# Row maxima of the first batch from float32 keys and queries, and a prologue written out in a new order, in an attention and expert kernel

## What is computed

```
def reference(x, ctx_1024, mask_Bx1x1xS2_fk0, ...):
    # attention of layernorm(x) over ctx: 16 heads of 16
    q = split_heads(layernorm(x) @ Wq + bq); k = split_heads(ctx @ Wk + bk); v = split_heads(ctx @ Wv + bv)
    logits = einsum('bhqd,bhkd->bhqk', q, k) / sqrt(16) + mask * -1e9
    x = x + merge(softmax(logits) @ v) @ Wo + bo
    # router and experts
    scores = softmax(layernorm(x) @ w_gate); weights, idx = top_k(scores, 2)
    x = x + sum over k of weights[k] * expert[idx[k]](layernorm(x))     # capacity 1024
```

## Time and profile before

| | us |
|---|---|
| median of 3 runs | 433.39 (429.33 to 435.75) |
| the profiled execution | 432.8 |
| its span, first to last instruction | 430.7 |
| TensorE, VectorE, ScalarE busy | 370.0, 248.4, 214.0 |

### The profile page before, as it was taken

The page is one execution under the profiler, slowest core; times in us unless marked ns, Lnnn a source line. Parts: engine busy times, 40 slices in busy tenths (PEclk is TensorE's granted clock), DMA queues, the critical chain, the costliest instruction groups (busy, mean ns, idle before and its releaser), DMA issues.

```text
span 430.7 us, 9281 instructions
## 1 busy us (share of the span) xinstructions
PE 370.0 (86%) x2752; PEld 292.7 (68%) x2753; DVE 248.4 (58%) x693; ACT 214.0 (50%) x342; POOL 165.7 (38%) x174
## 2 busy tenths in 40 slices
PE   5437895898899999998988599989899999999990
PEld 3324663565566656665654399878699999999980
DVE  4636656589988988887878356752233332333320
ACT  2620474557466665744446568534244454544440
POOL 5020152342747658241253005742233334243332
PEclk9956699899999999999999699999899999999997
DMA  6589259387784949487136213554432332424330
GB/s 201 123 197 191 53 178 187 132 187 198 162 201 173 202 166 206 131 187 190 50 137 215 82 50 62 130 107 87 73 62 46 62 48 47 73 42 73 51 56 4
DMA packets 65468, 51.93 MB, mean 121 GB/s; under 512 B 11898, under 2 KB 62346, under 8 KB 65418
## 3 DMA queue, kind: packets, MB, share of 16 engines
q1 hardware_dynamic: 58028, 42.71, 40.6%
q0 software_dynamic: 7008, 8.43, 12.0%
q10 hardware_dynamic: 400, 0.40, 0.3%
HBM read 32.89 MB, written 19.06 MB: 121 GB/s over the span
## 4 chain that ended last, share of the span: by engine, by line
PE 55%; DMA 18%; DVE 9%; issue 7%; SPq 6%; ACT 3%; POOL 1%; POOLq 0%; ACTq 0%; DVEq 0%
PE bank L1032 19%; PE bank L1043 9%; DMA out<-CTt,GG 7%; PE bank L987 5%; DVE NEG L1170 5%; PE bank L875 5%; PE bank L958 4%; PE bank L919 3%; PE bank L892 3%; DMA wf<-NMT 3%; DMA wf<-qparts_d 3%; PE bank L971 3%; PE bank L883 2%; DMA slots<-R,slot 2%; PE bank L1012 2%
## 5 line engine op out<-in xcount | busy, mean ns | idle before, releaser
L1032 PEld LDWEIGHTS bank<-CX,KS 128*128 128x128 f32 x912 | 109.0, 194 | 6.4 <-issue 4.7
L1032 PE MATMUL bank<-CX,KS 128*128 128x128 f32 x912 | 109.9, 278 | 2.4 <-issue 2.3
L1170 DVE TENSOR_REDUCE NEG<-bank 128x2 f32<-128x512 f32 x128 | 85.7, 685 | 35.7 <-PE bank L958 34.3
L761 ACT ACTIVATE PR<-bank 128x512 f32<-128x512 f32 x128 | 73.2, 591 | 47.2 <-PE bank L971 46.5
L665 POOL DMA_INDIRECT out<-CTt,GG x38 | 58.9, 1549 | 97.6 <-DMA out<-CTt,GG 60.8
L801 ACT ACTIVATE KS<-wf 128x1536 f32 x40 | 59.2, 1483 | 43.1 <-PE bank L1032 42.6
L1398 DVE COPY CX<-bank 128x256 f32<-128x256 f32 x39 | 16.5, 424 | 77.2 <-PE bank L1012 77.2
L958 PE MATMUL bank<-KS,wf 99*128 99x256 bf16 x224 | 45.6, 290 | 15.9 <-DMA wf<-qparts_d 10.2
L1043 PE MATMUL bank<-wp,QF 128*128 x228 | 56.9, 386 | 2.4 <-DVE CTt L1412 2.4
L584 POOL DMA_INDIRECT slots<-R,slot x32 | 32.7, 1022 | 38.0 <-DVE slot L1276 26.5
L971 PE MATMUL bank<-wf,KS 102*128 102x256 bf16 x224 | 43.2, 273 | 3.9 <-DMA wf<-NMT 3.2
(11 more groups left out here) (171 smaller groups left out, 466.4 us busy)
## 6 DMA issues: line engine op xcount, KB each, us to landing
wf<-in_L_ffn_c_fc SPq DMA_DIRECT2D x8, 768.0 KB, 5.2
XG<-slots SPq DMA_DIRECT2D x40, 128.0 KB
kparts_d<-KP SPq DMA_DIRECT2D x8, 384.0 KB, 2.5
KS<-kparts_d SPq DMA_DIRECT2D x8, 384.0 KB
KS<-kparts_d SPq DMA_DIRECT2D x24, 128.0 KB
qparts_d<-QP SPq DMA_DIRECT2D x8, 384.0 KB, 3.1
wp<-in_L_ffn_c_proj SPq DMA_DIRECT2D x8, 384.0 KB, 4.9
wf<-qparts_d SPq DMA_DIRECT2D x7, 384.0 KB
```

What stands on the lines that cost most here:

```text
L761: act.activation(PR[:, s % NPROB, :], STB[s % 2][:], ACT.Exp).then_inc(exp_done, 1)
L1032: ins = pe.matmul(bank[2 + 2 * u + g][:, c * P:(c + 1) * P], UP[u][:, (k * 2 + g) * FF + c * P:(k * 2 + g) * FF + (c + 1) * P], XTG[:, u, ...
L1170: dve.tensor_reduce(NEG[:, n % 2, t, 2 * hp:2 * hp + 2], MXB[m % 2][:].rearrange("p (i s) -> p i s", i=2), AX.X, ALU.max, negate=True).the ...
```

## The change

Batch 0's row maxima no longer use the rows from DRAM. VectorE makes, from the float32 keys and queries of batch 0 in the layout of the projection, two copies each (`KZ`, `QZ`, in the space of later expert weights): in a group of 32 partitions, two heads, copy i keeps head i and has in the place of the other head the mask (`MK` on the keys' side, `mask_row` on the queries'). `direct_maxima` multiplies 32 partitions by 32 partitions, four groups into four banks, and `reduce_direct` takes the maxima. Its 32 matmuls take the place of the 32 of `row_max_logits(0, u)`. The rows of batch 0 are still made, for the logits.

Iterations -2 and -1 are gone. Each engine has a prologue written out by hand: order of loads, of projections, of parts. ScalarE issues the loads of mask and biases, the rows of `MK` and half 0 of the maxima's rows of batch 0. GpSimd makes the subtractions of batches 0 and 1. There are 14 matmuls with an unread result at the start. Batch 2 is projected from unit 0 of iteration 0 on (lead 0: CT 0, K 1, XT 5, Q 7, second parts 9 and 10), the 16 maxima of batch 1 are packed in units 5 to 15 (`FIRST_MAXIMA`), NM0 of batch 1 moves from unit 11 to 13. `stats1_of(3)` is taken ahead of VectorE's loop and was in iteration -1, `stats1_of(4)` moves to unit 15. X of batch 3 is loaded behind the query reads of batch 1, x of batches 4 to 7 in iteration 0 behind the reads of batch 2 and ahead of `max_rows(1, 0)`. The reads and writes of SyncE in the iterations are as before, in functions with new names.

```diff
-    "second K of the first": 2, "second Q of the first": 8, "start of 1": 7, "lead": 7, "lead of 2": 4,
+    "lead": 7, "lead of 2": 0,
...
-ITERATIONS = range(-2, B)
+ITERATIONS = range(B)
+FIRST_MISC = [("CT", 0), ("K", 0), ("XT", 0), ("Q", 0), ("CT", 1), ("XT", 1), ("K", 1), ("Q", 1), ("NM0", 0), ("V", 0)]
+AT_FIRST = {"NM0": 13, "split 0": 11, "stats1": 15}
+FIRST_MAXIMA = {5: 1, 6: 1, 7: 2, 8: 1, 9: 2, 10: 1, 11: 1, 12: 2, 13: 1, 14: 2, 15: 2}
+GROUPS = 4
...
+def maxima_at(it, u):
+
+    if it + 1 >= B:
+        return ()
+    if it > 0:
+        return (u,)
+    first = sum(FIRST_MAXIMA.get(w, 0) for w in range(u))
+    return range(first, first + FIRST_MAXIMA.get(u, 0))
...
+        DIRECT = (bank[0], bank[1], bank[4], bank[5])
...
+        KZ = ZSPACE[:, 0:2 * KC * S].rearrange("p (i c s) -> p i c s", i=2, c=KC)
+        QZ = ZSPACE[:, 2 * KC * S:4 * KC * S].rearrange("p (i c s) -> p i c s", i=2, c=KC)
+        MK = ZSPACE[:, 4 * KC * S:4 * KC * S + 2 * S].rearrange("p (i s) -> p i s", i=2)
...
-            sp.dma_start(bkc[:], bk.rearrange("(c p) -> p c", p=P), allow_slow_non_contiguous=True).then_inc(wk_in, 16)
+            load_rows(1)
...
-            load_rows(1)
             sp.dma_start(wv[:], Wv.rearrange("(k p) n -> p k n", p=P)).then_inc(wv_in, 16)
-            load_rows(2)
...
+            load_rows(2)
...
+            load_output_weights(0)
+            sp.wait_ge(mask_out, 16)
+            mask_rows(0)
+            mask_rows(1)
+            write_keys(0)
+            load_output_weights(1)
+            write_queries(0)
+            read_keys(0)
+            read_queries(0)
+            write_keys(1)
+            load_context(2)
+            write_queries(1)
+            read_keys(1)
+            load_output_weights(2)
+            read_queries(1)
+            load_rows(3)
+            load_output_weights(3)
+            load_router()
+            load_context(3)
             for it in ITERATIONS[:-1]:
-                if 0 <= it:
-                    max_rows(it, 1)
+                max_rows(it, 1)
...
+                if it == 0:
                     for m in range(4, B):
                         load_rows(m)
+                max_rows(it + 1, 0)
+                if it + 4 < B:
+                    load_context(it + 4)
+                load_weights(it)
...
+            pool.memset(MK, 0.0).then_inc(mk_zero, 1)
+            pool.wait_ge(mk_zero, 1)
...
+            layernorm1(0)
...
-            layernorm1(0)
             layernorm1(1)
+            split_keys(pool, 0)
+            split_queries(pool, 0)
+            split(pool, 1)
+            layernorm1(2)
+            normalize1(pool, 2)
...
+            act.dma_start(maskrow[:], mask.rearrange("b i j s -> b (i j s)")).then_inc(mask_in, 16)
+            act.dma_start(bkc[:], bk.rearrange("(c p) -> p c", p=P), allow_slow_non_contiguous=True).then_inc(bk_in, 16)
+            act.dma_start(bqc[:], bq.rearrange("(c p) -> p c", p=P), allow_slow_non_contiguous=True).then_inc(bq_in, 16)
...
+            for i in range(2):
+                act.dma_start(MK[DH * (1 - i):P:2 * DH, i, :],
+                              mask.rearrange("b i j s -> b (i j s)")[0:1, :].broadcast_to([GROUPS, S])).then_inc(mk_in, 16)
...
+                        if n == 0 and kind == "Q" and c == 0:
+                            ins.then_inc(q_half, 1)
...
+            evacuate("CT", 0)
+            evacuate("K", 0)
+            evacuate("XT", 0)
+            first_part("K", 0)
+            second_of_keys(0)
+            evacuate("Q", 0)
+            first_part("Q", 0)
+            evacuate("CT", 1)
+            evacuate("XT", 1)
+            second_of_queries(0)
+            evacuate("K", 1)
+            first_part("K", 1)
+            evacuate("Q", 1)
+            second_of_keys(1)
+            evacuate("NM0", 0)
+            act.wait_ge(nmt_ready[0], 1)
+            for j in range(3):
+                act.dma_start(query_rows(0)[R_MAX + j:R_MAX + j + 1, 0:8, :],
+                              NMT[8 * j:8 * j + 8, 0, :]).then_inc(nm_in[0], 16)
+            first_part("Q", 1)
+            second_of_queries(1)
+            evacuate("V", 0)
...
+                    pe.wait_ge(mx_reduced, UNITS)
...
+            def direct_maxima(c, t):
+
+                first = GROUPS * (TB * c + t)
+                if t == 0:
+                    pe.wait_ge(qz_ready, 2 * (c + 1))
+                if first == 0:
+                    pe.wait_ge(kz_ready, 2)
+                for i in range(2):
+                    for g in range(GROUPS):
+                        if i == 0 and first > 0:
+                            pe.wait_ge(mx_reduced, first - GROUPS + g + 1)
+                        rows = slice(2 * DH * g, 2 * DH * (g + 1))
+                        ins = pe.matmul(DIRECT[g][:, i * S:(i + 1) * S], QZ[rows, i, c, t * P:(t + 1) * P], KZ[rows, i, c, :],
+                                        start=True, stop=True)
+                        if i == 1:
+                            ins.then_inc(mx_ready, 1)
+
+            def unread(count):
+                for _ in range(count):
+                    pe.matmul(STB[0][:, 0:P], ident[:], ident[:], start=True, stop=True)
+
             pe.wait_ge(const_step, CONST_IDENT)
+            unread(8)
+            misc("CT", 0)
+            unread(6)
+            misc("K", 0)
+            misc("XT", 0)
+            misc("Q", 0)
+            misc("CT", 1)
+            misc("XT", 1)
+            direct_maxima(0, 0)
+            misc("K", 1)
+            direct_maxima(0, 1)
+            misc("Q", 1)
+            direct_maxima(1, 0)
+            misc("NM0", 0)
+            direct_maxima(1, 1)
+            misc("V", 0)
...
+            def keys_by_head():
+
+                dve.wait_ge(kf_ready, 1)
+                dve.wait_ge(mk_in, 32)
+                for i in range(2):
+                    dve.scalar_tensor_tensor(out=KZ[:, i], in0=by_chunk(KF[:, 0, :]), scalar=own_head[:, i:i + 1],
+                                             in1=MK[:, i, :].unsqueeze(1).broadcast_to([P, KC, S]),
+                                             op0=ALU.mult, op1=ALU.add).then_inc(kz_ready, 1)
+
+            def queries_by_head(c):
+
+                dve.wait_ge(qf_ready if c else q_half, 1)
+                for i in range(2):
+                    dve.tensor_scalar(QZ[:, i, c, :], QF[:, 0, c * S:(c + 1) * S], own_head[:, i:i + 1],
+                                      mask_row[:, 1 - i:2 - i], ALU.mult, ALU.add).then_inc(qz_ready, 1)
...
+            keys_by_head()
...
+            queries_by_head(0)
+            queries_by_head(1)
...
+            def reduce_direct(c, t):
+                for g in range(GROUPS):
+                    m, hp = GROUPS * (TB * c + t) + g, GROUPS * c + g
+                    dve.wait_ge(mx_ready, m + 1)
+                    dve.tensor_reduce(NEG[:, 0, t, 2 * hp:2 * hp + 2],
+                                      DIRECT[g][:].rearrange("p (i s) -> p i s", i=2), AX.X, ALU.max,
+                                      negate=True).then_inc(mx_reduced, 1)
...
+            reduce_direct(0, 0)
+            reduce_direct(0, 1)
+            split_max(0, 0)
+            reduce_direct(1, 0)
+            reduce_direct(1, 1)
+            dve.memset(VA[:, :, :, :, DH:32], 1.0).then_inc(va_ones, 1)
+            dve.wait_ge(const_step, CONST_ALL)
...
+            stats1_of(2)
+            stats1_of(3)
             for it in ITERATIONS[:-1]:
                 for u in range(UNITS):
-                    if 0 <= it + 1 < B:
-                        reduce_max(it + 1, u)
-                    if u == AT["split 1"] and 0 <= it < B:
+                    for w in maxima_at(it, u):
+                        reduce_max(it + 1, w)
```

More of the change, by code:

```diff
@@ L92, with place @@
 UNREAD = {(B - 3, 9): 0, (B - 3, 11): 1, (B - 2, 0): 2, (B - 2, 9): 3, (B - 2, 11): 4}
-ITERATIONS = range(-2, B)
+ITERATIONS = range(B)
[3 more added lines that the diff above has]
+GROUPS = 4
+def place(kind, it):
+    return AT_FIRST.get(kind, AT[kind]) if it == 0 else AT[kind]
+def maxima_at(it, u):
[5 more added lines that the diff above has]
+    return range(first, first + FIRST_MAXIMA.get(u, 0))
 def projected(it):
-    if it == -2:
-        return (0, 1)
-    return (it + 2,) if 0 <= it < B - 2 else ()
+    return (it + 2,) if it < B - 2 else ()
 def start_unit(n):
-    if n < 2:
-        return UNITS * -2 + n * AT["start of 1"]
     return UNITS * (n - 2) - (AT["lead of 2"] if n == 2 else AT["lead"])
 def projected_at(it, unit, after):
-    return [n for n in range(B) if start_unit(n) + after == UNITS * it + unit]
+    return [n for n in range(2, B) if start_unit(n) + after == UNITS * it + unit]
 def second_at(it, unit, kind):
-    return ([n for n in projected_at(it, unit, AT[kind + " of the first"]) if n < 2] +
-            [n for n in projected_at(it, unit, AT[kind]) if n >= 2])
+    return projected_at(it, unit, AT[kind])
 def misc_at(it, unit):
@@ L127, in misc_at @@
         pieces.append(("UNREAD", UNREAD[it, unit]))
```

(20 more changed lines are left out.)

153 lines of the change are left out of this document (72 added, 81 removed).

## The result

The changed kernel takes 438.14 us (median of 4 runs, 434.59 to 440.11) against 431.83 us for the kernel before on the same chip (4 runs, 429.33 to 435.75): a ratio of 1.018, with a 95% interval of 1.010 to 1.026. Its profiled execution is the fastest of its four, 434.59 us with a span of 432.8; before it was 432.8 us with 430.7. So of the 6 us between the medians the two traces show 2.1 at their ends, and more in the middle.

The account below looks back on a forecast made before the run. The bound was taken as the head's chain of DRAM row transfers, setting iteration 1's first logits, with a fixed sequence behind. These move from 76.18 to 82.0, +5.8 us: span 436.5, time 438.6, median 439, range 436 to 442.

Parts of the forecast that it names:

- the case that I gave the highest chance: The forecast itself: 439 us, within 436 to 442, chance 0.50.
- The maxima's gain stands in VectorE's wait: Iteration 0: the 17 us won on batch 0's maxima stand idle while VectorE waits for x of batch 3.
- Batch 2 is late by its place in the units: Iteration 0: later units put the write of batch 2's keys at 62.7 (before 60.87), its rows at 77.7.
- The four loads hold back the maxima's rows: Before iteration 1: x of batches 4 to 7 delays the maxima's rows by 4.0 + 0.3 us, to 82.0.
- Rival B: Before iteration 1: the four loads don't delay the maxima's rows; start at 77.7, +1.5, 435 us; chance 0.20.
- The prologue's terms: Head: keys 0 at 9.2, direct tiles at 15, reductions end at 24, keys 1 written at 27.2.
- both my bounds: Direct maxima: 32 row-group matmuls on TensorE take from 2.1 us (column-group pace) to 7.6 us (full matmuls in sequence).
- rival C: Prologue itself slow: keys 1 later than 29.5 delays everything behind one for one; 441 to 448 us, chance 0.15.
- C's two conditions: Prologue: K0 and Q0 run on the slow clock (+2.0 us each), or the row groups don't overlap (+5.5).
- Iteration 1: From iteration 1's first logits to iteration 2's: 25.2 us as before, give or take 1.
- The sum: Span 430.7 + 5.8 = 436.5 us, own time 2.1 more, 438.6; the median 439.
- Rival A: Iteration 0: the maxima's gain comes through, iteration 1 at 74.3, 1.9 us earlier; 424 to 432 us, chance 0.15.

Follow-up runs that it names:

- e1: Changed kernel with x of batch 3 issued behind x of batch 2 in SyncE's prologue, not behind batch 1's query reads: 434.15 us, 0.995 of the kernel before.
- e4: Changed kernel with VectorE taking batch 3's statistics in unit 9 of iteration 0, all transfers left in place: 434.99 us, 0.999 of the kernel before.
- E5: Changed kernel with both loads of x moved earlier and batch 2's XT, Q, second parts in units 2 to 5: 420.62 us, 0.973 of the kernel before.
- e8: Changed kernel with only batch 2's XT, Q and second parts moved to units 2 to 5 of iteration 0: 432.39 us, 1.003 of the kernel before.
- e2: Changed kernel with x of batches 4 to 7 issued right behind max_rows(0, 1) in iteration 0: 436.33 us, 1.005 of the kernel before.
- e3: Changed kernel with x of batch 3 issued early and x of batches 4 to 7 behind max_rows(0, 1): 431.36 us, 0.989 of the kernel before.
- b1: Kernel before with x of batches 4 to 7 between batch 2's reads and max_rows(1, 0), stats1_of(4) in unit 15: 433.57 us, 1.0035 of the kernel before.
- E6: Changed kernel with ScalarE copying Q1's first part ahead of NM0 and its three issues: 435.19 us, 1.008 of the kernel before.
- The second series: The changed kernel run again unedited, beside later experiments on the same chip: 435.72 us, 1.010 of the kernel before.

## Why the prediction was right, and where its terms were off

The forecast was 439 us, the median is 438.14, within the range, and the case that I gave the highest chance is the one that happened. Its steps in turn:

**The maxima's gain stands in VectorE's wait.** Forecast: x of batch 3 at 44.5, NM1 at 46.7. Measured 47.04 and 48.97. Two experiments show it from two sides: with the load moved (e1) or the statistics moved (e4), the wait is gone and iteration 1 starts 7 to 9 us earlier. That is what the wait was worth, and not 17 us: of these e1 keeps 12.3 at the first maxima of batch 1 (45.03 for 57.35), which wait for their rows, and 3.7 at iteration 1 (72.50 for 76.18).

**Batch 2 is late by its place in the units.** Forecast: unit 5 at 51.3, keys 2 at 62.7, rows at 77.7. Measured 53.53, 63.88 and 77.74. The last agrees by luck. Unit 5 was 2.2 us late (2.3 of it by NM1), from there to the write it took 10.35 us for 11.4 forecast, and from the write to the rows 13.9 for the 15.0 of before: errors of 1 to 2 us that cancel. E5 and e8 show that the place is what sets it.

**The four loads hold back the maxima's rows.** Forecast 4.3 us between rows and logits. Measured 3.5, of which 0.4 to 0.6 stay without the loads (e2, e3): their price is 3.0. The traces of e2, e3 and b1 show it; the times of e2 and b1 alone don't. Rival B (the loads don't matter) has fallen by the traces. The Trainium skill, "DMA: Bandwidth & Descriptors", "Queues, rings and completion order", says of the completion of transfers that it is "not FIFO per issuing engine". In the seven traces with the 1 MB between them in which TensorE waits for both, the 12 KB of rows issued behind it were waited for 2.5 to 3.6 us beyond batch 2's rows, and in the changed kernel the pieces landed in the order of issue (x at 78.2 to 80.5, the rows at 81.16), so for this kernel the in-order reading of the ring, which the same section gives, describes the time.

**The prologue's terms.** Keys 0 at 9.66 (9.2), the first direct tile at 16.08 (15). From there it is off: the last reduction ends at 31.5 and not at 24. For the row groups both my bounds were half of what they should be, since I took the doubled listing for the number of matmuls: by the 8 matmuls on column groups in 1.07 us it is 4.3 for 32 and not 2.1, by full ones (4 in 1.89 us, 0.47 each) 15.1 and not 7.6. Eight took 1.15 us at a listed clock of 1.00, so 4.6 for 32: my choice of the low end was right, its number not. The last eight, which wait for banks, are spread over 3.86 us at a mean clock of 0.67. What set the pace of the reductions is TensorE's order: K1 and Q1 stand between the groups of maxima (3.53 and 1.99 us), and I had let the reductions run one after another, bound by VectorE alone. VectorE waited 1.98 us for the second group and 1.32 for the last. The wrong term with the largest effect is the write of keys 1, 31.36 for 27.2: ScalarE copied Q1's first part at 28.36 to 28.99, behind three issues from 26.20 on, where I had 24.1 to 24.7. Batch 0's rows were late too (31.1 for 29.5), and the DMA engines, for which I had forecast no hole from 18 to 44, stood empty from 31 to 32 (share 0.00). This is the price that rival C names, 1.9 us past its point of 29.5, but not by C's two conditions: K0 and Q0 were not slow (1.89 and 1.99), and the row groups overlap. The next steps are late by as much or a little more (batch 1's rows at 46.0 for 43.5, x of batch 3 at 47.0 for 44.5). E6 got 2.4 to 3 us back in the trace. So a slow prologue is in the result, with a price at the low end of what I gave it, and the errors that cancel in batch 2 hid it.

**Iteration 1.** 25.2 us was carried over from before; measured 26.2. Its Q3 starts right after TensorE's idle time, at the lower clock: 3.4 us in the chain of waits, where the kernel before had 2.9 at the same place and Q2 took 1.7. That is 0.5 of the 1.0 us; of the rest, 0.4 is a wait for the maxima's rows at the start of iteration 2 (107.38). Hence the shift of 5.0 us at iteration 1 and 6.0 at iteration 2.

**The sum.** 436.5 of span were forecast, 432.8 measured in the profiled execution, 432.9 to 438.7 in other executions of the same kernel. I added the shift of iteration 1 to the end unchanged ("everything is a fixed sequence"). In this trace only 2.1 of 5.0 us reach the end, and the profiled execution is the fastest of its four, so the trace and the median disagree by more than the forecast and the median do. The second series puts the effect at 1.0%, 436 on the 431.83 of the first. Between 1 and 2% the sum can't be judged closer; that the forecast is within 1 us of one median is chance.

**Rival A** (the gain comes through) fell for this kernel, by the order of the code. Its working was right in its kind: I put a gain of over 2% at keys 2 written by 48.5 and said it would take batch 1's rows in half the time. E5 has it with 51.02, without faster reads, by placing the batch in earlier units. That way out I hadn't seen.

## What to carry to other kernels

When a long wait is taken out of an in-order queue, list what each engine has next behind its waits. Here a load that nobody needed for another 18 us, waited for on the one engine that also prepares the next step, held everything up by 7 to 9 us. Work saved at the head is worth something only if the next long chain (parts, write, read back) starts earlier too: place the next batch's pieces for the new time, and put large loads that aren't urgent into the hole of the DMA engines and not between a read and the small transfer that the path waits for. Count matmuls in the code before pricing them from a list that shows each of them twice.

## What the runs showed that I had not expected

**The lower clock (1.2 GHz, listed as 0.50) costs the first projection behind a wait, and in some executions one without a long wait.** V1 after the 10.28 us of waiting took 3.62 us, Q3 at the start of iteration 1 as long, and K1 in the middle of the direct maxima 3.53, each for the matmuls of a projection that take 1.9 to 2.0 at the higher level (2.4 GHz, granted 1.00). For K1 the profile's clock is 0.54 from 17.3 to 20.7, and 1.00 again in the next group of maxima, in the first two of the stretches above; TensorE had idled for 1.7 us at most since 13.5. In the second trace of the changed kernel it is 1.00 in the same stretch, behind the same work. Two traces of one kernel can so differ by more than a small edit moves them.

**Row groups overlap nearly in full.** Eight float32 matmuls of 32 rows and 256 columns on four groups take 1.15 us, that is 0.14 each, against 0.47 for a full one at the same clock (a projection's four take 1.89): 3.3 times as fast, on four groups. The 8 on column groups that make the product with values take 1.07.

**GpSimd's subtraction of 512 columns takes 1.16 us for VectorE's 0.69**, as I had counted, and three transfers issued by ScalarE take 2.06 us of its queue, as they do of SyncE's.
